# Second half's row transfer issued by POOL, four value products behind the turn's quarters, and VectorE's division inside the turn

## The reference, cut to what matters

```python
xn = _layernorm(x, axis=-1)
s = _L0_attn_ref(xn, wq, wk, wv, wo)          # softmax(q k / 4 + causal mask) v, then wo
g = _silu(_L0_ffn_ref(xn, W_gate, b_gate, W_e, b_e))   # mean of the two chosen experts' relu(x W_e + b_e)
x = x + s * g
```

## Time and profile before

| | |
|---|---|
| median of 3 runs | 668.13 us (668.01 to 669.14) |
| the profiled execution | 668.61 us, of which the span of instructions is 666.9 us |
| first turn product of group 1 to that of group 31 | at 126.61 to 545.16 |
| PE busy | 626.9 us, 94% of the span |
| DVE busy | 550.6 us, 83% |
| ACT busy | 287.4 us, 43% |
| POOL busy | 237.8 us, 36% |
| mean granted TensorE clock | 0.990 of full speed |

### The profile page before, as it was taken

The page is one execution under the profiler, slowest core; times in us unless marked ns, Lnnn a source line. Parts: engine busy times, 40 slices in busy tenths (PEclk is TensorE's granted clock), DMA queues, the critical chain, the costliest instruction groups (busy, mean ns, idle before and its releaser), DMA issues.

```text
span 666.9 us, 12169 instructions
## 1 busy us (share of the span) xinstructions
PE 626.9 (94%) x3539; PEld 339.3 (51%) x3565; DVE 550.6 (83%) x1789; ACT 287.4 (43%) x535; POOL 237.8 (36%) x364
## 2 busy tenths in 40 slices
PE   8899998998999999999999998999999999699997
PEld 5788784433433334333434343443443443378886
DVE  6698999869987788978988788897789976589994
ACT  4343325434444344434544434443454444444441
POOL 3777642333322212322222322222232115576620
PEclk9999999969999999999999999999999999989999
DMA  7599988879799565594863748658276527668841
GB/s 261 141 325 303 319 230 171 148 157 282 149 290 168 151 130 83 134 194 139 176 117 86 154 109 200 132 164 152 54 163 109 172 81 253 135 150 223 208 107 67
DMA packets 79902, 113.10 MB, mean 170 GB/s; under 512 B 9704, under 2 KB 42664, under 8 KB 79840
## 3 DMA queue, kind: packets, MB, share of 16 engines
q1 hardware_dynamic: 68098, 86.90, 53.3%
q0 software_dynamic: 6704, 18.62, 11.5%
q10 hardware_dynamic: 5038, 6.84, 4.2%
HBM read 72.15 MB, written 39.65 MB: 168 GB/s over the span
## 4 chain that ended last, share of the span: by engine, by line
PE 48%; DVE 23%; DMA 12%; issue 5%; SPq 5%; POOL 2%; ACT 2%; ACTq 1%; DVEq 0%; POOLq 0%
DVE bank L1398 11%; PE bank L1676 10%; PE bank L1025 8%; PE bank L2166 6%; PE bank L1596 5%; DMA qt<-m_rows 4%; PE bank L2171 4%; PE bank L1687 3%; PE bank L1648 3%; DMA qt<-turned_parts 3%; DMA w_e<-expert_rows,slots 3%; PE bank L1622 2%; SPq L1312 2%; DMA arena<-gathered_rows 2%; SPq L1313 2%
## 5 line engine op out<-in xcount | busy, mean ns | idle before, releaser
L1398 DVE CUSTOM_DVE_ANT_0 bank<-bank,cst 128x384 f32<-128x384 f32 (+3 forms) x512 | 235.0, 521 | 47.9 <-PE bank L1596 46.6
L1519 ACT ACTIVATE arena<-bank 128x512 f32<-128x512 f32 x320 | 171.0, 599 | 182.6 <-PE bank L1622 83.6
L1336 POOL TENSOR_SCALAR_AFFINE_SELECT arena<-arena 128x512 f32<-128x512 f32 x128 | 80.5, 642 | 312.0 <-ACT arena L1519 312.0
L1676 PE MATMUL bank<-w_e,arena 128*128 x312 | 161.0, 622 | 4.3 <-issue 4.1
L1596 PE MATMUL bank<-kt,qt 48*128 48x512 f32 (+1 forms) x496 | 110.1, 337 | 5.7 <-DVE arena L1398 3.8
L1596 PEld LDWEIGHTS bank<-kt,qt 48*128 48x128 f32 x496 | 69.2, 187 | 84.5 <-DVE arena L1398 51.0
L1648 PE MATMUL bank<-arena 128*32 128x512 f32 (+3 forms) x1024 | 89.7, 447 | 5.7 <-ACT arena L1519 3.6
L1622 PE MATMUL bank<-qt,kt 50*128 50x512 f32 x256 | 87.4, 454 | 2.6 <-DMA qt<-m_rows 1.9
L1676 PEld LDWEIGHTS bank<-w_e,arena 128*128 128x128 f32 x312 | 54.1, 192 | 58.4 <-issue 55.6
L1398 DVE DVE_READ_ACCUMULATOR2_ANT arena<- 128x1 f32 x512 | 71.9, 140 | 0.0
L1687 PE MATMUL bank<-w_proj,arena 128*128 128x512 f32 x128 | 66.5, 627 | 0.0
(11 more groups left out here) (168 smaller groups left out, 935.7 us busy)
## 6 DMA issues: line engine op xcount, KB each, us to landing
qt<-turned_parts SPq DMA_DIRECT2D x96, 128.0 KB, 5.0
turned_parts<-qk_parts SPq DMA_DIRECT2D x8, 1280.0 KB, 7.1
gathered_rows<-s_tok SPq DMA_DIRECT2D x39, 256.0 KB, 5.9
arena<-gathered_rows SPq DMA_DIRECT2D x39, 256.0 KB, 3.3
expert_rows<-arena SPq DMA_DIRECT2D x39, 256.0 KB, 5.7
w_e<-in_L_ffn_W_e ACTq DMA_DIRECT2D x24, 256.0 KB, 6.0
kt<-turned_parts SPq DMA_DIRECT2D x96, 64.0 KB, 4.6
arena<-in_L_attn_x SPq DMA_DIRECT2D x16, 256.0 KB, 5.0
```

What stands on the lines that cost most here:

```text
L1336: g.affine_select(out=diag, in_=diag, compare_op=ALU.is_ge, fill=0.0, base=0, pattern=[[0, 2], [0, HALF], [1, P]], channel_multiplier=-1). ...
L1398: i = v.tensor_tensor_reduce(out=part, in0=part, in1=const("mask")[:, S - w:], scale=1.0, scalar=LOWEST, op0=ALU.add, op1=ALU.max, accum_o ...
L1519: nc.scalar.activation(pt[:, s, first:second + 1:second - first].rearrange("p c r q -> p c (r q)"), s2_bank(b, h, n).rearrange("p (c x) -> ...
L1676: i = t.matmul(bank[7], xgt[:, m % 2, k * P:(k + 1) * P], w_e[:, ex[m], k, :], start=False, stop=(k == KB - 1))
```

## The change

Three things are changed in the chain of turns.

1. POOL issues the second half's row transfer, behind its four selects and ahead of the gather of slot 2, for groups 2 to 31. ACT no longer does. The second half gets its own semaphore, `b_mr1`, so that the first piece of `scores_2` waits for SP's half alone and the second piece for POOL's.
2. All four value products stand behind gap 3. SIX becomes (1, 1, 2, 2, 0) and EIGHT (2, 2, 2, 2, 0); turn 30 goes from (2, 2, 1, 1, 0) to (1, 1, 2, 2, 0). The number of quarters of each turn stays.
3. On DVE `normalise` moves from behind maxima 0 and 1 to between `maxima_columns` and `maxima_rows`, `pair_rows` to right behind `maxima_rows`, and `expert_x` of slot 0 from ahead of `maxima_rows` to behind `pair_rows`.

```diff
-SIX, EIGHT = (2, 1, 1, 1, 1), (2, 2, 1, 1, 2)
+SIX, EIGHT = (1, 1, 2, 2, 0), (2, 2, 2, 2, 0)
-SIZES = [NONE, (0, 0, 0, 2, 2)] + [SIX, EIGHT] * 12 + [SIX, SIX] + [SIX, EIGHT, (2, 2, 1, 1, 0), NONE]
+SIZES = [NONE, (0, 0, 0, 2, 2)] + [SIX, EIGHT] * 12 + [SIX, SIX] + [SIX, EIGHT, (1, 1, 2, 2, 0), NONE]
...
+        def rows_in(b, h, s):
+            g = b * NG + h + 1
+            return 16 * (g + min(g, 2)) if s == 0 else 16 * (g - 2)
...
-            e.dma_start(qt[...].bitcast(F32), m_rows[...].bitcast(F32)).then_inc(b_mr, 16)
+            e.dma_start(qt[...].bitcast(F32), m_rows[...].bitcast(F32)).then_inc(b_mr if s == 0 or b * NG + h < 2 else b_mr1, 16)
...
                     select(b, h, 1)
+                    if 0 < b * NG + h < NB * NG - 1:
+                        maximum_rows(e, *next_group(b, h, 1), 1)
                     next_gather(b, h, 2)
...
+                    if later:
+                        normalise(*done)
+                    if following:
+                        maxima_rows(e, st, *following)
+                    if later and done[1] % 2:
+                        pair_rows(done[0], done[1] // 2)
                     for m in TURNS.get((b, h, 0), ()):
                         expert_x(m)
-                    if following:
-                        maxima_rows(e, st, *following)
                     if after:
                         for n in (0, 1):
                             maxima(e, *after, n)
-                    if later:
-                        divided(*done)
...
                     results(b, h, 2)
-                    if b * NG + h + 1 < NB * NG:
-                        maximum_rows(e, *next_group(b, h, 1), 1)
                     for n in (8, 9):
                         exps(e, b, h, n)
...
-                e.wait_ge(b_mr, nth_of(32, b, h, 32))
+                e.wait_ge(b_mr, rows_in(b, h, 0))
+            if n == 1 and b * NG + h > 1:
+                e.wait_ge(b_mr1, rows_in(b, h, 1))
...
-                    values(e, b, h, 0)
                     quarters(b, h, 2)
                     turn_maxima(e, *following)
                     scores(e, (0, 1), after, (8, 9), (b, h))
                     quarters(b, h, 3)
-                    for j in ORDER[1:]:
+                    for j in ORDER:
                         values(e, b, h, j)
                     quarters(b, h, 4)
```

More of the change, by code:

```diff
@@ L1237, in build @@
         b_v = sem("b_v")
-        b_tm, b_me, b_mr = sem("b_tm"), sem("b_me"), sem("b_mr")
+        b_tm, b_me, b_mr, b_mr1 = sem("b_tm"), sem("b_me"), sem("b_mr"), sem("b_mr1")
         b_s1, b_m, b_mx = sem("b_s1"), sem("b_m"), sem("b_mx")
@@ L1318, in maximum_rows @@
             at = 64 * s + ROWS
-            e.dma_start(qt[at:at + 2, h // 2 % 2, h % 2].bitcast(F32), m_rows[64 * s:64 * s + 2 * HALF * TPB].bitcast(F32)).then_inc(b_mr, 16)
+            e.dma_start(qt[at:at + 2, h // 2 % 2, h % 2].bitcast(F32), m_rows[64 * s:64 * s + 2 * HALF * TPB].bitcast(F32)).then_inc(b_mr if s == 0 or b * NG + h < 2 else b_mr1, 16)
         def pool_b(e, st):
@@ L1412, in maxima_rows @@
             e.wait_ge(b_tm, nth_of(1, b, h, 1))
-            if due(at := nth_of(32, b, h, 0)):
-                e.wait_ge(b_mr, at)
+            for s, rows in enumerate((b_mr, b_mr1)):
+                if b * NG + h > 2 * s:
+                    e.wait_ge(rows, rows_in(b, h - 1, s))
             v.tensor_copy(m_high[:, :], turned_at(b, h)).then_inc(dve_steps, st.one())
```

## The result

The changed kernel takes 683.41 us (median of 4 runs, 680.38 to 684.56), the kernel before, run beside it, 668.07 (667.10 to 669.14): a ratio of 1.0222, 95% interval 1.0200 to 1.0244. It is slower by 15.3 us; the forecast was 1.6 faster, and its range ended at 674. The profiled execution took 684.32, its span 682.6; the mean granted TensorE clock is 0.972 (0.990 before).

The account below looks back on a forecast made before the run. PE was taken as close to the bound, its tails and EIGHT heads setting the time directly, SIX heads following DVE's chain. Terms from +8.0 (class C) to -3.8 (class E) summed to -1.6: 667.0 profiled, 666.5 median; range 661.5 to 674.

Parts of the forecast that it names:

- plain tail: PE behind the turn product, with two quarters and four value products joined and no waits: 5.07 us.
- classes B and F: EIGHT tails of turns 9, 13, 17, 25 (20.3, -2.1) and 5, 21, which had waited for row transfers (10.1, -2.4).
- C tails: SIX tails of turns 2, 6, 14, 22, 28, where an expert's tile begins: 6.7 each, 33.5, +8.0.
- Class E: SIX tails of turns 4, 12, 20 with a late expert load: its wait moves behind the row parts, 15.2, -3.8.
- The row transfers' risk of +1.7: Slow row transfers in odd turns: 5.0 worse in all if they stay at 5.3, a third of it taken.
- POOL's half: Rival, chance 0.08: POOL's row transfer lands late at the second piece of scores_2; +23, 689.
- the copy of the maxima in SIX heads: Nine SIX heads, copy .57 beside POOL's selects: selects end about where the copy starts, 7.7 each, -3.1.
- the key and query loads: Loads start as before, but even turns ask for them some .5 earlier: +1.0, bounds 0 and 3.5.
- A SIX head is as long as DVE's chain of maxima, whatever PE does in it: SIX heads: turn products wait for DVE's copy of the maxima, still by over 1 us after the change.
- D: EIGHT tails of turns 3, 7, 11, 15, 19, 23, 29, waiting for expert's rows: 5.97 each, 41.8, -1.0.
- The reason for F: Turns 5, 21: POOL's gather stood ahead of the row transfer; with it behind, transfers may become quick, -2.4.
- transfers still set the turns: Rival, chance 0.26: row transfers still over 4 us in odd turns hold up a turn's first scores; 672.3.

Follow-up runs that it names:

- the last pair of ratios: loads_and_two_undone against the kernel before, .9877 (659.25 us), and the same with ACT issuing the second half's row transfer, .9852 (659.11 us).
- pool_issue_undone: Changed kernel with ACT issuing the second half's row transfer again, POOL's gather ahead of the row parts: 677.81 us, ratio 1.0165.
- half_loads: Changed kernel without the first half's key and query loads behind turn 3, old data used again: 671.68 us, ratio 1.0062.
- loads_each_turn: Changed kernel with key and query loads split by turn, the second turn's twelve issued one turn later, same bytes: 672.89 us, ratio 1.0075.
- quarters_undone: Changed kernel with the quarters and value product 0 where they were before: 669.50 us, ratio 1.0003.
- batch_turns_2112: Changed kernel with a quarter moved from gap 2 to gap 0 in turns 8, 16 and 24: 683.75 us, ratio 1.0249.
- loads_and_two_undone: loads_each_turn with DVE's order of before and the quarters of batch_turns_2112: 659.25 us, ratio 0.9877 to the kernel before.
- division_undone: Changed kernel with DVE's order of before (expert_x, row parts, two maxima, then division and pair's rows): 677.82 us, ratio 1.0179.

## Why the prediction was wrong

**Right.** The plain tail (.87 + 1.92 + 2.28) is 5.07 in classes B and F. The expert's rows, the item that spoke most against the change, came as told in kind: C tails were put at 6.7, and turns 6, 22 and 28 are 6.70, 6.70 and 6.69. Class E, told as 15.2, is 15.40 once the loads are in time. EIGHT heads -2.4 (told -2.8), nine and three SIX heads -4.5 (told -3.1), turn 30's head -1.0 (told -.7). The row transfers' risk of +1.7 did not come, and POOL's half was not late: the thirty transfers land after 2.1 at the median. POOL takes .58 to .67 to issue one, where .955 was taken.

```profile
qt<-m_rows POOLq DMA_DIRECT2D x30, 8.0 KB, 2.1
```

The Trainium skill ("SBUF — State Buffer", section "SBUF: two separate sides") warns that a DMA issued by GpSimd can starve while VectorE holds the shared port, 3100 ns in its example. This row shows no sign of that, but does not test it: as the prediction has it, mostly transposes and maxima of VectorE stand behind the row parts, not copies or casts. The Trainium skill's rule in "DMA: Bandwidth & Descriptors", section "Issuing engines are not separate DMA queues", that another issuer saves only issue time, fits the last pair of ratios, .9877 and .9852, with their wide intervals. With the loads late the issuer made 3.8 us of difference (`pool_issue_undone`), but there POOL's gather moved too.

**Misread: the copy of the maxima in SIX heads.** I set .57 beside selects against .18, as if the short copies ran clear of POOL. They do not: in turn 20 the copy runs from 407.10 to 407.28 and the two selects from 406.53 to 407.77. The long ones end .03 behind the second select (turn 22: 436.83 behind 436.79). After the change they still do (446.23 behind 446.21), but last .29 in place of .57. So the heads gained although the selects did not move clear of the copy, and that the sum should then be 3.1 higher did not hold.

**The step that failed: the key and query loads, "+1.0 (bounds 0 and 3.5)".** I had "loads start as before, but even turns now ask for them some .5 earlier". From the issues and PE's first scores of the traces, by pair: before, the loads were needed 11.2 to 13.3 behind their first issue, and where PE waited for them they were there after 11.7 to 12.9. After, in ten of thirteen pairs they are needed 10.9 to 11.8 behind it, and are there after 11.5 to 12.7. In turn 10 the time to need fell from 11.92 to 11.21, in turn 14 from 12.05 to 10.92; in the ten pairs it fell by .9 in the mean, where I had .5. Turn 10 in the two traces, before and after: the first issue, then the turn product; the scores need the loads some .2 behind its start, and had them only at 275.95 in the second.

```profile
257.83 0.32 SPq L1312 DMA_DIRECT2D kt<-turned_parts  x1
269.55 0.33 PE L1633 MATMUL bank<-cst,arena 128*128 128x128 f32 x1 [0.32 <-DVE arena L1407]
...
263.31 0.32 SPq L1312 DMA_DIRECT2D kt<-turned_parts  x1
274.32 0.33 PE L1643 MATMUL bank<-cst,arena 128*128 128x128 f32 x1 [0.50 <-DVE arena L1414]
```

The loads take what they took; the two shorter pieces between issue and need, an odd tail and an even head, had been their cover, with nothing to spare. So what the change wins there comes back as a wait: PE's waits for loads rose from 1.7 to 8.3, by 6.6 where the term had 1.0 and at most 3.5. That bound was of the wait only; the clock behind it was in no term. `half_loads` and `loads_each_turn` show what hangs on the loads in the changed kernel, 11.7 and 10.5 us (10.7 and 9.8 by the ratios), some three times my upper bound; with them in time it takes 671.68 and 672.89, inside the range of the forecast. Two things limit this reading. Loads in time gain 5.3 on the kernel before as well, so that in the difference between the two kernels the loads stand for 5.2 of the 10.5 (an estimate from the medians). And in the trace of `quarters_undone` such waits come without part 2 too, in a kernel that loses nothing.

**Not seen: the heads of turns 8, 16 and 24**, +5.2. "A SIX head is as long as DVE's chain of maxima, whatever PE does in it" holds only while PE has work until DVE's maxima come. In these turns the division stands amid the maxima, and the quarter that left gap 0 had covered it. PE stood 1.26, the clock fell, and the two quarters that the change put into gap 2 made PE the last. `batch_turns_2112` shows it: 9.07 each. Of the 31.39, 31.39 - 3 x 9.07 = 4.2 went with that.

**Mis-sized: the experts' rows in odd turns.** I had them 1.77 behind the turn product, for a copy that ends .15 ahead of it. In turn 7 the quarter starts 2.12 behind it, and D is 44.46, not 41.8: seven times .35 and a little. Of the .35, .09 is the copy, which ends .06 ahead, .11 the way from the copy to the end of the transpose (2.03, told 1.92), and .15 from that end to the quarter's start, which was in no term. `loads_and_two_undone` and `division_undone` take this wait away, 36.8.

**The reason for F was wrong** though its 10.14 was told as 10.1: `pool_issue_undone`. What made those row transfers slow before, and lets turn 5's be slow in both kernels with ACT's issue and loads in every turn (1.20 and 3.39 of wait), stays open.

**Of the rivals,** "transfers still set the turns" named the right place, the first scores of a turn's tail, and the wrong transfer: row transfers for the bulk, loads for 2.5.

**The sum in other terms.** Where a window at full clock can be compared with one that is not, the clock alone cost about 8.7: 4.2 in the three heads, 1.0 in the tail behind turn 8's head, 1.6 in turn 10 (8.13 less the plain 5.07 and the 1.43 by which the loads came late) and 1.9 in turn 14 (8.64 against 6.70). It is part of the terms above, not a further one. What decides that the clock falls behind one wait and not another was not tried: in `loads_each_turn` the tails of turns 6 and 28 have the same wait for experts' rows, 1.18, and the heads of 8, 16 and 24 the same 1.25 to 1.26:

```profile
212.46:219.16 6.70, 5.52 (x43) 2.11 (x43) 4.99 (x13) 1.68 (x3) 0.66 (x1) 1.00 0.59 151
...
517.99:526.33 8.34, 7.16 (x43) 2.40 (x43) 5.45 (x19) 1.51 (x3) 0.66 (x1) 0.80 0.41 123
...
233.82:243.90 10.08, 8.43 (x36) 3.90 (x33) 8.23 (x33) 4.95 (x9) 3.11 (x5) 0.86 0.46 136
345.65:354.71 9.06, 7.21 (x36) 3.38 (x32) 8.24 (x33) 4.94 (x9) 3.11 (x5) 1.00 0.51 147
456.16:466.51 10.35, 8.71 (x36) 4.11 (x33) 8.23 (x33) 4.94 (x9) 3.12 (x5) 0.84 0.41 129
```

## What to carry to other kernels

When you shorten a stretch, list every transfer that is issued ahead of it and needed behind it, and hold the time from issue to need, before and after, against what the transfer takes: here it fell from some 12 us to 11 with 12 wanted. Put a mend into the kernel before as well: the loads in time gained there too, so that only a part of what they gain in the changed kernel explains why it is slower. Give idle time on a busy TensorE a price above its length, for the work behind it may run at half the clock. And when one mend moves nothing, look at where its gain was given back before you call it wrong: the quarters for turns 8, 16, 24 and DVE's order moved 0 and 5.6 us by themselves, and 13.6 together once the loads were in time.

## What the hardware showed that I had not expected

A wait of 1.2 to 1.3 us on PE cost nothing beyond itself in some places and 1.0 to 1.6 more in others, in the same program: 9.06 and 10.35 for two heads with equal waits, at granted clocks of 1.00 and .84. And splitting the loads evenly over the turns, with the same bytes in twice as many transfers, made the kernel before 0.8% faster.
